# One stream of projection, attention and finish in 64x32 tiles, both score groups of a unit ahead of its weighting, in place of three stages

## What is computed

```python
qkv = einsum('bse,fe->bsf', layernorm(x), in_proj_weight) + in_proj_bias
scores = einsum('bhqd,bhkd->bhqk', q * 0.25, k)
scores = where((j <= i) & (j >= i - 16), -inf, scores)
out = einsum('bse,fe->bsf', softmax(scores) @ v, out_proj_weight) + out_proj_bias
x = x + out
x = x + tanh(layernorm(x) @ W @ A1 @ A2 + bias)
```

## Time and profile before

| | us |
|---|---|
| median of 3 runs (lowest, highest) | 2341.0 (2338.85, 2341.24) |
| the profiled execution | 2342.14 |
| its span, first to last instruction | 2340.4 |
| TensorE matmul busy | 2137.5 (91%) |
| ScalarE busy | 1985.3 (85%) |
| DVE busy | 925.9 (40%) |
| GpSimd busy | 112.2 (5%) |
| mean granted TensorE clock | 0.979 of full |
| transfers | 139.56 MB, 60 GB/s |

### The profile page before, as it was taken

One profiled execution on the slowest core, in us unless ns is written; L12 is line 12 of the kernel. 1 busy time (PEld: TensorE's weight loads), 2 busy tenths in 40 slices (PEclk: granted clock), 3 DMA queues, 4 the chain that ended last, 5 costly groups with the idle time before them and its releaser, 6 DMA issues. The chain is left out here.

```text
span 2340.4 us, 39058 instructions
## 1 busy us (share of the span) xinstructions
PE 2137.5 (91%) x13648; PEld 543.5 (23%) x13648; DVE 925.9 (40%) x1768; ACT 1985.3 (85%) x1578; POOL 112.2 (5%) x127
## 2 busy tenths in 40 slices
PE   6899899999999999999999999999999999995887
PEld 3555111111111111111111111111111111111665
DVE  6887133223232323242424242333233333332887
ACT  3444899989999999899999998999999989995112
POOL 3211000000000000000000000000000000000332
PEclk9999899999999999999999999999999999998999
DMA  6799302020202020203020202020212011001453
GB/s 197 258 304 327 54 8 48 8 49 8 48 8 49 8 49 8 49 6 50 7 50 5 51 6 38 19 45 11 31 26 34 22 20 36 6 5 54 127 158 99
DMA packets 86859, 139.56 MB, mean 60 GB/s; under 512 B 11152, under 2 KB 53520, under 8 KB 84624
## 3 DMA queue, kind: packets, MB, share of 16 engines
q1 hardware_dynamic: 86672, 137.02, 23.7%
HBM read 69.60 MB, written 67.37 MB: 59 GB/s over the span
## 5 line engine op out<-in xcount | busy, mean ns | idle before, releaser
L698 ACT ACTIVATE probs<-scores 128x1536 f32<-128x1536 f32 x1368 | 1853.5, 1455 | 57.8 <-PE outs L671 23.3
L671 PE MATMUL outs<-probs,vs 128*32 128x512 f32 x8192 | 1103.9, 611 | 1.1 <-DVE probs L730 0.9
L658 PE MATMUL scores<-qs,ks 49*128 49x512 f16 x4096 | 829.9, 387 | 112.4 <-ACT probs L698 101.8
L730 DVE TENSOR_TENSOR probs<-probs,allowed 128x288 f32<-128x288 f32 (+2 forms) x608 | 232.6, 408 | 991.8 <-ACT probs L698 990.8
L658 PEld LDWEIGHTS scores<-qs,ks 49*128 49x128 f16 x4096 | 151.0, 93 | 1152.3 <-ACT probs L698 1112.0
L671 PEld LDWEIGHTS outs<-probs,vs 128*32 128x32 f32 x8192 | 162.5, 108 | 444.2 <-issue 340.2
L716 DVE RECIPROCAL inverse<-inverse 128x512 f32<-128x512 f32 x64 | 214.6, 3353 | 2.2
L456 ACT ACTIVATE qk_f<-ps_qk,bias_qk 128x512 f32<-128x512 f32 x64 | 44.0, 688 | 105.3 <-PE ps_qk L499 90.2
L1224 ACT ACTIVATE squashed<-pre 128x1024 f32<-128x1024 f32 x16 | 16.9, 1057 | 127.7 <-DVE pre L1205 127.7
L711 DVE LOAD_MASK_SELECT sums<-outs x64 | 0.9, 14 | 299.6 <-PE outs L671 299.6
L499 PE MATMUL ps_qk<-xt,w_qkv 128*128 128x512 f32 x256 | 114.1, 598 | 0.9 <-issue 0.9
(11 more groups left out here) (70 smaller groups left out, 658.2 us busy)
## 6 DMA issues: line engine op xcount, KB each, us to landing
qk_full<-qk_f SPq DMA_DIRECT2D x64, 256.0 KB, 3.3
v_ones<-vaug SPq DMA_DIRECT2D x16, 1024.0 KB, 5.1
vs<-v_ones SPq DMA_DIRECT2D x16, 1024.0 KB
qs<-q_parts SPq DMA_DIRECT2D x96, 128.0 KB
ks<-k_parts SPq DMA_DIRECT2D x96, 128.0 KB
xin<-in_x SPq DMA_DIRECT2D x16, 512.0 KB, 6.0
q_parts<-parts SPq DMA_DIRECT2D x32, 256.0 KB, 2.8
k_parts<-parts SPq DMA_DIRECT2D x32, 256.0 KB, 3.1
```

The costliest lines, as they stand in the source:

```text
L658: last = pe.matmul(scores[:, bank], ks[rows, par, unit, kb * P:(kb + 1) * P], qs[rows, par, unit, qc * CHUNK:(qc + 1) * CHUNK], start=True ...
L671: last = pe.matmul(outs[32 * h:32 * h + 32, s % 2], vs[:, par, kb, h], probs[:, (u * HG + h) % RING], start=(kb == 0), stop=(kb == KBS - 1))
L698: act.activation(prob_ring[:, b:b + cols], tile_ring[:, a:a + cols], ACT.Exp, scale=1.0 / (SCALE_UP * SCALE_UP)).then_inc(r.exped, 1)
L730: dve.tensor_tensor(tiles, tiles, keep_row, ALU.mult).then_inc(r.masked, 1)
```

## The change

Before the stream, `first_batch` projects the four chunks of batch 0 (as `project` did, but on 64-key tiles for v, without the float32 copy, with the key rows cleared in four large memsets on GpSimd). Then `stream` has 16 steps of 64 units, all unrolled. A step is a chunk of 512 queries; its units are 2 groups of 8 heads x 32 blocks of 64 keys. In a step the engines also project chunk `step + 4` (12 steps) and finish chunk `step - 1` (15 steps, the last behind the stream). The pieces of that work stand at fixed units `r` of TensorE's and DVE's lists. ScalarE does only exponentials and the tanh; its former copies go to DVE, its squares to GpSimd. The exact path is three blocks behind the stream (`exact_project`, `exact_attend`, `exact_finish`), each skipped on the flag, and projects again for itself.

All attention matmuls use tiles of 64 rows and 32 columns: 8 score matmuls fill the array and give two heads' banks for 4 key quarters, 8 weighting matmuls take 4 heads on 2 halves of the rows. Score banks are two slots of two. An exponential covers 1024 columns.

The normalisation no longer sits on DVE's wide tile: the sums go to DRAM (`move_context`), come back as 128x64, are inverted, go out, and come back in sixteen broadcasts (`invert_sums`); DVE then multiplies (L855).

```diff
+PASS_HEADS = HEADS // HALVES
+QUADS = PASS_HEADS // 2
+KEYS = HALF_P
+KBLOCKS = SEQ // KEYS
+RING = 8
+STEP = HALVES * KBLOCKS
...
+            for hg in range(HALVES):
+                for e in range(2):
+                    pool.memset(lay["ks"][e * HALF_P + 32:(e + 1) * HALF_P, hg * QUADS:(hg + 1) * QUADS],
+                                GUARD_K).then_inc(cleared, 1)
+                    pool.wait_ge(cleared, 4 + 2 * hg + e)
+            rsqrt(2)
...
+            for hg in range(HALVES):
+                load_queries(sp, lay, 0, hg, q_parts)
+                load_keys(sp, lay, 0, hg, k_parts)
+            sp.wait_ge(guard_done, 1)
+            sp.dma_start(guards[0], guard[:]).then_inc(guard_out, 16)
+            sp.wait_ge(guard_out, 16)
+            for hg in range(HALVES):
+                load_guards(sp, lay, 0, hg, guards)
...
+        def weighed_at(position):
+            i = position % KBLOCKS
+            base = position - i
+            if i < 3:
+                found = [base - 3 + i]
+            elif i == 3:
+                found = []
+            elif i < 13:
+                found = [position - 4]
+            elif i == 13:
+                found = [position - 4, position - 3]
+            else:
+                found = [position - 3]
+            return [u for u in found if 0 <= u < NCH * STEP]
...
+            def move_context(step, hg):
+                done = step * HALVES + hg + 1
+                sp.wait_ge(out_free, done)
...
+                for side in range(2):
+                    for c in range(HG):
+                        rows = slice((side * HG + c) * HD, (side * HG + c + 1) * HD)
+                        sp.dma_start(ctx_in[rows, hg], raw[32 * c:32 * c + HD, side]).then_inc(ctx_moved, 16)
+                    heads = slice(hg * PASS_HEADS + side * HG, hg * PASS_HEADS + (side + 1) * HG)
+                    sp.dma_start(row_sums[heads], raw[HD:P:32, side]).then_inc(sums_out, 16)
...
+            def invert_sums(step):
+                sp.wait_ge(sums_out, (step + 1) * 64)
+                sp.dma_start(sums[:], row_sums.rearrange("h (k t) -> (h k) t", t=64)).then_inc(sums_in, 16)
+                sp.wait_ge(inverted, step + 1)
...
+                for hg in range(HALVES):
+                    for h in range(PASS_HEADS):
+                        head = hg * PASS_HEADS + h
+                        sp.dma_start(inverse[h * HD:(h + 1) * HD, hg],
+                                     row_inverse[head].partition_broadcast(HD)).then_inc(inverse_in, 16)
...
+                for slot in range(2):
+                    act.wait_ge(scored, 2 * u + slot + 1)
+                    if slot == 0 and u >= RING:
+                        act.wait_ge(summed, u - RING + 1)
+                    act.activation(probs[:, u % RING, 2 * slot:2 * slot + 2].rearrange("p c q -> p (c q)"),
+                                   scores[:, 2 * slot:2 * slot + 2].rearrange("p c q -> p (c q)"),
+                                   ACT.Exp, scale=1.0 / (SCALE_UP * SCALE_UP)).then_inc(exped, 1)
+                if step and r == 60:
+                    squash(step - 1)
...
+            def score(u, slot):
...
+                if u:
+                    pe.wait_ge(exped, 2 * u + slot - 1)
+                for quarter in range(4):
...
+                    for e in range(2):
+                        rows = slice(e * HALF_P, e * HALF_P + FAST_ROWS)
+                        last = pe.matmul(scores[cols, 2 * slot + e], ks[rows, group, keys], qs[rows, group],
+                                         start=True, stop=True)
...
+                for c in range(HG):
+                    at = kb * V_ROW + (hg * HG + c) * V_COLS
+                    for side in range(2):
+                        keys = slice(side * HALF_P, (side + 1) * HALF_P)
+                        last = pe.matmul(outs[32 * c:32 * c + 32, side], vs[keys, at:at + 2 * HD],
+                                         probs[keys, u % RING, c], start=(i == 0), stop=(i == KBLOCKS - 1))
...
+                for r in range(STEP):
+                    u = step * STEP + r
+                    score(u, 0)
+                    score(u, 1)
+                    for w in weighed_at(u):
+                        weigh(w)
+                    if projects and r in (8, 9):
+                        turn(step, r - 8)
+                    if projects and r in (12, 14):
+                        project_qk(step, 0, (r - 12) // 2)
+                    if projects and r in (16, 18):
+                        project_qk(step, 1, (r - 16) // 2)
+                    if finishes and r in (20, 22, 24, 26):
+                        project_out(f, (r - 20) // 2)
+                    if projects and r in (28, 30):
+                        project_qk(step, 2, (r - 28) // 2)
+                    if projects and r in (32, 33):
+                        project_qk(step, 3, r - 32)
+                    if projects and r in (35, 37):
+                        project_v(step, (r - 35) // 2)
+                    if projects and r == 39:
+                        sum_squares(step)
+                    if finishes and r in (43, 44):
+                        f_turn(f, r - 43)
+                    if projects and r in (46, 48):
+                        project_v(step, 2 + (r - 46) // 2)
+                    if finishes and r in (50, 52, 54, 56):
+                        project_f(f, (r - 50) // 2)
```

1453 lines of the change are left out of this document (975 added, 478 removed).

## The result

| | before | changed |
|---|---|---|
| median of 4 runs, us (lowest, highest) | 2341.1 (2338.9, 2341.2) | 2427.0 (2425.0, 2431.6) |
| ratio, 95% interval | | 1.037 (1.035 to 1.039) |
| span of the profiled execution, us | 2340.4 | 2424.2 |
| first exponential to end of last, us | 240 to 2138 | 145.0 to 2361.5 |
| transfers, MB | 139.56 | 92.80 |

The forecast was 2410 us; the measured time lies 17 us above it, inside the range, on the side that had the chance of 0.76. That total hides larger errors which cancel, and the rows show each of them.

What follows compares the result with a forecast made beforehand. ScalarE's exponentials were taken to bound the attention. First batch 115, exponentials 1874, tanh 14, new ScalarE idle time 347 and tail 60 summed to 2410 us; range 2290 to 2490.

Steps and rivals of the forecast that it cites:

- the side that had the chance of 0.76: Whole kernel: the change was forecast slower than before with chance 0.76, faster 0.21, same 0.03.
- The step that decided it: TensorE's order in a unit: weighting and piece stand before the next scores; a piece delays the next exponential 1.08 us.
- Exponentials: ScalarE in the stream: 2048 exponentials of 1024 columns at 0.915 us each, 1874 us, bounds 1843 to 1966.
- Pieces, transposes, norms, double weightings: Extra TensorE work in the stream's units: 347 us of new idle time on ScalarE, bounds about 230 to 390.
- The spare time of 0.07 us: Unit without a piece: a TensorE chain of 1.76 us covered by 1.83 us of exponentials, leaving 0.07 us.
- the rival of serial row groups: Attention matmuls: two row groups don't run side by side, TensorE holds each unit 2.75 us, 3340 us; chance 0.03.
- the rival of instruction issue: TensorE in the stream: issuing 64 instructions a unit at 0.07 us each sets the time, 4780 us; chance 0.04.
- First batch: Front, four chunks projected ahead of the stream: first exponential at 115 us instead of 240, bounds 98 to 125.
- Tail: Behind the last exponential: remaining weighting, normalisation, finish and skipped exact stages take 60 us, bounds 48 to 70.
- Covered: DVE and SP work beside the stream adds no time; the broadcast chain ends about 31 us into a chunk.
- that rival: Late transfers or DVE: broadcasts end 5 us after the masks need them, 75 us over 15 chunks, 2485 us; chance 0.13.
- Cheaper pieces (2246): Stream's units: no stagger, free shape changes, spare time 0.19 us, a piece costs 0.73 us; 2246 us, chance 0.18.

Runs made afterwards that it cites:

- the order with both between: Changed kernel with weighting and piece both moved between the two score sets of a unit: 2429.6 us, ratio 1.038 to the kernel before.
- the short exponentials: Changed kernel with exponentials of 896 instead of 1024 columns, the ring filled with ones beforehand: 2325.2 us, ratio 0.995 to the kernel before.
- the kernel with the weighting between: Changed kernel with the weighting moved between the two score sets of a unit, the piece behind the second: 2266.9 us, ratio 0.971 to the kernel before.

## Why the prediction was right, and where only its sum was

*The step that decided it was right.* The prediction said that TensorE's order puts the weighting and a piece between the second score set of a unit and the next first one, and that such a piece delays the next exponential by 1.08 us. Measured is 2.91 - 1.82 = 1.09. The two orders with weighting and piece apart take the cost away and the order with both between keeps it. The chain is shown, not argued.

*Exponentials:* forecast 1874 us. Units without a piece take 1.82, so 1024 x 1.82 = 1864: 10 less. Halfway between two rows of other widths was good to 0.5%. By the formula of the Trainium skill (ScalarE: Activation LUTs, What ACT_TABLE_LOAD costs) it would have been 1937.

*Pieces, transposes, norms, double weightings:* forecast 347. Over the 1.82 us units, the first step has 131.3 - 116.5 = 14.8, the eleven full ones 140.3 - 116.5 - 0.9 of tanh = 22.9 each, the four that only finish 11.5 each: 15 + 252 + 46 = 313. The term was 34 too large. Two things are behind it, both in the code that was read: unit 35 has no weighting at all, so the piece of v there costs 0.19 instead of 1.08 (11 us over 12 steps); and I gave the cheaper price of a piece that follows another only to the twelve q/k pieces, while it also holds where a piece or transpose stands next to a double weighting or another transpose (units 13 and 14 cost 0.33 and 0.76 instead of 0.86 and 1.08, units 45 and 46 cost 0.59 and 0.62: 19 us over 12 steps).

*Sizes behind it:* two score sets take 0.44 us (1107.21 to 1107.65), so 0.22 each, the low end of my bounds; scores to exponential 0.48 instead of 0.53; a weighting to its end 0.98 with its change of shape, a piece 1.06 with its own. The spare time of 0.07 us, which every piece's price contains, came out by two errors that cancel. From the end of an exponential to the next unit's first one the chain is 0.05 + 0.22 + 0.87 + 0.48 = 1.62 us, not 1.76 (the short exponentials let a unit without a piece fall to 1.72 and 1.62). But what covers it isn't 1.83 either, since exponentials overlap: one ends at 1104.89, and the third behind it, unbroken, would start at 1105.68 + 0.91 = 1106.59, which is 1.70. So 0.08 is spare, and a piece costs 0.11 + 1.06 - 0.08 = 1.09. Matmuls of eight tiles do run side by side: the rival of serial row groups is excluded. So is the rival of instruction issue: 64 TensorE instructions fit into 1.82 us, 0.028 us each. The 62 ns that the Trainium skill (TensorE: Matmul & The Clock Gate, Wait — 56ns, not 53.3ns?) gives per matmul where microcode decodes would be 1.98 us for the 32 matmuls of a unit; here such a unit takes 1.82 and TensorE still waits in it.

*First batch:* forecast 115, measured 145.0. This is the step that failed. "The chunk is 16 us late" named the wrong victim: the memsets held DVE's normalising of the second chunk for 27.6 us, and the last part came at 102.8 instead of 92. The rest is the transfers: "guard store and landing 3.5" took 24 us, because I counted 24 loads by their issue (12 us) and not by their bytes, 3.8 MB that kept the DMA engines full until about 139 us. The clue for the first error was in the trace of before: there too the first chunk's normalising took 7.59 us for what is 1.4 in chunks without a memset beside it, while GpSimd cleared memory:

```profile
8.62 7.59 DVE L370 TENSOR_SCALAR xn<-xin,mean_var,rstd 128x256 f32<-128x256 f32 x4 [1.68 <-POOL rstd L310]
```
```profile
8.46 3.51 POOL L329 MEMSET vaug<- 128x4096 f32 x1
...
14.10 1.97 POOL L335 MEMSET ks<- 32x2048 f16 x1
```

DVE ends at 16.21, the last memset at 16.07. I had read the group for its length only.

*Tail:* forecast 60, measured 2424.2 - 2361.5 = 62.7.

*Covered:* the chain of broadcasts was forecast to end 31 us into a chunk. The scaling starts 27.5 to 30.5 us into most chunks and 34 to 35 into three, ahead of the output piece each time; that rival stayed empty. Not forecast were the stalls at batch ends, 25 us.

The sum against 2410: front +30, exponentials -10, pieces -34, stalls +25, tail +3, together +14, and the span was 2424.2. (The "356 us of attention time" in the forecast is a slip: from 1898 to 2235 it is 337, and the sum of 2410 doesn't use it.) The two misses of 30 and 25 us had no place in my bounds of their own terms (the front was to lie between 98 and 125); the pieces, priced too high, hid them. That the total came within 17 us is luck. The sign is not: without those 55 us the kernel would still have taken about 2372 us, slower than before. What carried it was the unit's chain and its count.

*Cheaper pieces (2246)* was the rival on the other side. Its sizes were the right ones (score set 0.22, weighting 0.87, ready near 0.50). Its spare time of 0.19 us was not (0.08 above), nor its free change of shape: from its start to the next instruction's a weighting takes 0.98 us ahead of a piece and 0.87 ahead of a score set of its own shape (1035.69 to 1036.56 in the kernel with the weighting between), so the change ahead of a piece costs about 0.1 us; the one behind it is in the piece's 1.06. These two rows are of that kernel:

```profile
1035.69 1.04 PE L1140 MATMUL outs<-probs,vs 64*32 64x512 f32 x16
1036.56 0.40 PE L1121 MATMUL scores<-qs,ks 49*32 49x512 f16 x8
```

## What to carry to other kernels

When two engines hand a buffer of two slots back and forth, look at what stands in each of the two intervals between the hand-overs, not at the sum: work that fits when it is spread over both costs its full length when it stands in one. Price a batch of loads by its bytes as well as by its issues, and ask what small transfer stands behind it. In a long unrolled program like this one, look for stalls that nothing releases wherever the DMA engines are full. And before putting a long memset on GpSimd, look what DVE does in that time.

## What the runs showed of the hardware

- Four normalising instructions of DVE that met four GpSimd memsets of 7.0 us each took 6.5 to 7.1 us each, one for every memset: 27.56 us for 1.4 us of work. In the kernel with word-wide memsets they met shorter ones, and took 11.48.
- A memset of 32 x 8192 float16 takes 6.99 us on GpSimd (27.95 / 4) and 8.65 us from start to start on DVE, whose row shows 6.88. As 4096 float32 words GpSimd needs 3.57 us.
- 24 loads, 3.8 MB in all (12 of 64 KB and 12 of 256 KB), keep the DMA engines full for about 30 us at 116 to 131 GB/s. A small store behind them lands 24 us after its issue, and within 3.3 us where only six of the 64 KB loads stand ahead of it.
- Beside queued loads that fill the DMA engines, TensorE in unrolled code stopped for 3 to 5 us at a time. In the stall that begins at 1795.6 its granted clock went from 1.00 to 0.50 and was back at 1.00 at 1804.4, with matmuls running again from 1800.75. With one 256 KB load in flight at a time no stall is longer than 1.0 us.
